# Sync queue of a gated cross-attention kernel: the load of the next second half of the stacks stands ahead of the store of the second half's maxima

## The reference, cut to what matters

```
q = rope(Wq @ layernorm(x) + bq); k = rope(Wk @ ctx + bk); v = Wv @ ctx + bv     # (16, 8, 512, 16) each
p = softmax(q k^T / sqrt(16)); x = x + tanh(g0) * (Wo @ (p v) + bo)
h = silu(layernorm(x) @ Wgate) * (layernorm(x) @ Wup); y = h @ Wdown
x = x + tanh(g1) * y / rms(y)
```

## Time and profile before

| | value |
|---|---|
| median of three runs | 773.88 us |
| profiled execution | 772.05 us, of which 770.2 us are the span from the first to the last instruction |
| TensorE | 697.0 us busy, 90% of the span |
| VectorE, ScalarE, GpSimd | 611.6, 524.3 and 471.9 us busy |
| DMA | 84.79 MB, mean 110 GB/s; the attention stage moves 150 to 219 GB/s in most slices |
| load of a half, one of its two transfers | 384 KB, 60 issues, median 6.3 us from issue to landing |

### The profile page before, as it was taken

How to read it: one execution, slowest core, us unless ns; L and a number is a source line. 1 busy time by engine, 2 the same in 40 slices (tenths; PEclk the granted TensorE clock), 3 DMA queues, 4 the chain that set the end, 5 groups by cost and what they waited for, 6 DMA issues and landing times. The chain is left out here.

```text
span 770.2 us, 13361 instructions
## 1 busy us (share of the span) xinstructions
PE 697.0 (90%) x4660; PEld 337.8 (44%) x4660; DVE 611.6 (79%) x822; ACT 524.3 (68%) x929; POOL 471.9 (61%) x399
## 2 busy tenths in 40 slices
PE   3589999989999999999999914899999999999995
PEld 1234443433444334433444303456655655565553
DVE  6689988859888889878888206877789888987894
ACT  2038888858888888878888813666675667566663
POOL 3935675656667866786421102796679668866762
PEclk9559999979999999999999966999999999999998
DMA  6787777877777787776851132000000200000011
GB/s 219 195 199 182 175 163 195 202 175 179 199 188 179 176 200 187 192 159 150 199 109 45 38 112 102 0 1 1 1 0 15 97 0 1 29 29 0 2 42 68
DMA packets 51047, 84.79 MB, mean 110 GB/s; under 512 B 14500, under 2 KB 17956, under 8 KB 50980
## 3 DMA queue, kind: packets, MB, share of 16 engines
q1 hardware_dynamic: 49680, 82.93, 42.5%
q10 hardware_dynamic: 1300, 1.01, 0.5%
HBM read 47.21 MB, written 34.34 MB: 106 GB/s over the span
## 5 line engine op out<-in xcount | busy, mean ns | idle before, releaser
L695 DVE TENSOR_REDUCE max_rows<-s_ps 128x2 f32<-128x1024 f32 x256 | 306.2, 1214 | 56.4 <-PE s_ps L440 55.2
L542 ACT ACTIVATE probs<-st_ps 128x512 f32<-128x512 f32 x512 | 277.4, 595 | 74.1 <-PE st_ps L452 64.0
L1088 ACT ACTIVATE parts<-gu_ps,gu_sc 128x512 f32<-128x512 f32 x176 | 118.0, 685 | 86.0 <-PE gu_ps L1176 85.9
L470 PE MATMUL pv_ps<-probs,v_ones 128*32 128x256 f32 x2048 | 164.9, 395 | 2.2 <-ACT pv_sb L548 2.2
L1062 POOL TENSOR_TENSOR pair<-parts 128x512 f32<-128x512 f32 x88 | 119.1, 1356 | 75.9 <-ACT parts L1088 75.5
L440 PE MATMUL s_ps<-qk_stack 48*128 48x512 f32 x512 | 134.6, 523 | 15.3 <-DMA qk_stack<-image 7.7
L1176 PE MATMUL gu_ps<-x_head,gu_bits 128*128 128x512 f16 x352 | 134.1, 381 | 4.1 <-DVE up L940 1.8
L1176 PE MATMUL gu_ps<-x_rest,gu_bits 128*128 128x512 f16 x352 | 133.4, 379 | 0.0
L452 PE MATMUL st_ps<-qk_stack 50*128 50x512 f32 x512 | 109.6, 417 | 0.5 <-DMA qk_stack<-max_scratch 0.4
L943 DVE SCALAR_TENSOR_TENSOR up<-gu_ps,gu_sc,up 128x512 f32<-128x512 f32 x132 | 98.8, 748 | 9.5
L440 PEld LDWEIGHTS s_ps<-qk_stack 48*128 48x128 f32 x512 | 50.0, 192 | 124.9 <-issue 76.5
(11 more groups left out here) (103 smaller groups left out, 852.0 us busy)
## 6 DMA issues: line engine op xcount, KB each, us to landing
qk_stack<-image SPq DMA_DIRECT2D x60, 384.0 KB, 6.3
image<-split_head SPq DMA_DIRECT2D x31, 256.0 KB
image<-split_head SPq DMA_DIRECT2D x62, 128.0 KB
image<-split_rest SPq DMA_DIRECT2D x31, 256.0 KB
ct<-ctx_dram SPq DMA_DIRECT2D x16, 256.0 KB, 4.3
scale_of<-inverse_scratch SPq DMA_DIRECT2D x16, 256.0 KB
xg<-x_scratch SPq DMA_DIRECT2D x4, 1024.0 KB, 7.2
out_dram<-y_out SPq DMA_DIRECT2D x16, 256.0 KB, 2.0
```

Of the source, the lines that this page charges most:

```text
L470: last = nc.tensor.matmul(pv_ps[2 * KC * j:2 * KC * (j + 1), cols], v_ones[b % 2][:, kt, j, quad, :], probs[at % PROBS][:, j, cols], start ...
L542: nc.scalar.activation(probs[at % PROBS][:, tile % 4, :], st_ps[item % ST_BANKS][:], ACT.Exp).then_inc(st_read, 1)
L695: nc.vector.tensor_reduce(out, s_ps[item % S_BANKS][:], AXIS_X, ALU.max).then_inc(s_read, 1)
L1088: nc.scalar.activation(parts[T_ % 2][:, k], gu_ps[(2 * k) % BANKS][:], ACT.Copy, scale=gu_sc[:, k, T_ % IT:T_ % IT + 1]).then_inc(gate_rea ...
```

## The change

In `sync_step` the store of the maxima of half 1 changes places with the load of half 1 of the next element. No instruction is added or taken away; the waits go with their functions.

```
 def sync_step(sp, b):
     nxt, proj_n = b + 1 < B, b + AHEAD_PROJ
-    store_max(sp, b, 1)
     if nxt:
         load_half(sp, b + 1, 1)
+    store_max(sp, b, 1)
     if b:
         gather_sums(sp, b - 1, 1)
     load_max(sp, b, 1)
```

## The result

The changed kernel takes 811.13 us (median; 805.21 to 818.34), against 773.19 us before: a ratio of 1.043 (95% interval 1.035 to 1.050), 33 us slower on 772. The forecast of 798 us had the sign, the place and the mechanism of the late store; the loss, 33 us by the ratio and 38 us by the medians, is 8 to 13 us larger than its 24.8 us. The time stays 0.9 us under the upper end of the stated range and lies just outside the 784 to 811 us of the forecast's own case: that it is inside the range at all is partly luck.

A forecast was written before the change was run, and what follows sets the result against it. A ring of sync queue and GpSimd, turning once per step, was taken as the bound. Seven turns (18.9 us), two with weight loads (2.8) and other steps (3.1) add 24.8 us to 772.05; with 1.8 for the median, 798 us, range 779 to 812.

The forecast's parts named there:

- the forecast's own case: Whole kernel: slower through the store's late return, forecast 798 us, own range 784 to 811 us, chance 0.62.
- The ring: Sync queue and GpSimd wait on each other, one turn per step, steps 3 to 12; a turn gets 2.7 us longer.
- The store behind the load: Sync queue: the store returns only once the load ahead has landed, so the load of the maxima goes 5.8 us late.
- The rival in which the store overtakes the load: Sync queue: store back before the load lands, its delay falls into idle time; 768 us (764 to 774), chance 0.09.
- The rival of a load that is quick once it is first: Sync queue: load lands within 4.5 us, store back at about 210.5; 768 us, chance 0.03.
- What the queue swallows: Sync queue, step 6: idle times of 2.26 and 1.51 us absorb part of the delay; broadcast issued 2.1 us late.
- The failed step: Sync queue, from the store of the inverses to the broadcast into `scale_of`: almost no gap, broadcast issued 2.1 us late.
- The open term: Landing of the broadcast into `scale_of`: 2.7 us late, between 2.1 us and 3.6 us.
- the second end: Broadcast landing set by the load of the first half, if bytes queued behind it keep engines full: 3.6 us late.
- the first rival: TensorE: its clock falls too after longer waits, five falls bring 798 to 808; 802 to 816 us, chance 0.12.
- Its counterargument: TensorE at slot 8: against a clock fall, the wait splits into two, at `score` and at `weigh`.
- Ahead of and behind the turns: Steps 12 and 13 add 1.3 us each at slot 8, step 2 some 0.5 us: 3.1 us.

The follow-up runs named there:

- experiment 8: Kernel before, with the load of the down scales moved behind the next step's load of the second half's maxima: 767.90 us, ratio 0.989.
- experiment 7: Changed kernel, with the load of the down scales moved behind the next step's load of the second half's maxima: 785.54 us, ratio 1.018 to the kernel before.
- experiment 9: Kernel before, with the load put first in steps 0 to 2 and 13 to 15 alone, old order in steps 3 to 12: ratio 1.002.
- experiment 4: Changed kernel, with the store of the second half's maxima issued from ScalarE's queue, behind the exponentials of slot 1: 780.16 us, ratio 1.001 to the kernel before.
- experiment 12: Kernel before, store first, with an added sync queue wait for the second half's load to land before the load of the maxima: 817.14 us, ratio 1.043.
- experiment 5: Changed kernel, with the load of the second half's maxima moved behind the merges and input loads: 812.84 us, ratio 1.038 to the kernel before.
- experiment 6: Changed kernel, with the store of the inverses moved ahead of the load of the first half: 816.02 us, ratio 1.050 to the kernel before.
- experiments 3: Changed kernel, with four throw-away products before the wait for the maxima at slot 8 of steps 3 to 13: 803.79 us, ratio 1.032 to the kernel before.
- experiment 10: Changed kernel, with four throw-away products before each of the two waits at slot 8 of steps 3 to 13: 806.75 us, ratio 1.035 to the kernel before.
- experiment 2: Changed kernel, with the store of the maxima placed between the load's two transfers: 791.33 us, ratio 1.013 to the kernel before.
- experiment 1: Changed kernel run again with no edit: 810.79 us, ratio 1.042 to the kernel before.
- experiment 11: Kernel before, load of the down scales moved as in experiment 8, two weight loads moved to steps 13 and 14 behind the input loads: 759.90 us, ratio 0.977.

## Why the prediction was right, and where it was short

*The ring.* Shown from both sides, for a third to a half of the loss: opening it gains 1.1% without the change (experiment 8) and brings the reorder's price from 4.3% down to 2.3 or 2.9% (experiment 7 against 8); the reorder outside it costs nothing that shows (experiment 9). The forecast put nearly the whole loss on the ring. With the ring open the queue's own issues and waits fill a step of 26.5 us, and that it did not see.

*The store behind the load.* Right in place and size: the load of the maxima was put 5.8 us late, and is 8.15 less 2.37, 5.8 us late (3.7 to 6.6 us over the nine turns, each against the same step before). The rival in which the store overtakes the load is out: in three of the nine turns the load of the maxima leaves 0.3 to 0.7 us before the load's second transfer has landed, in the other six 0.2 to 0.3 us after it. From another queue the store comes back no earlier when the load stands ahead of it (experiment 4). The rival of a load that is quick once it is first is out too: 7.5 us, as before. The Trainium skill gives the fit that the forecast set beside it ("DMA: Bandwidth & Descriptors", "Anatomy of one DMA") for transfers issued from GpSimd, and the load goes out on the sync queue, so the row decides. By experiment 12 the late load of the maxima, with the queue standing still ahead of it, is enough to explain the whole ratio. The Trainium skill, "DMA: Bandwidth & Descriptors", section "Queues, rings and completion order", gives each of the two issuing queues its own rings on the same 16 engines, each consumed in order, with the engines taking turns between rings. From that one would expect a store on the other queue to come back ahead of the load; the trace of experiment 4 does not show it, within 0.5 us in all six steps.

*What the queue swallows.* The store of the next maxima is 3.5 us late (3.6 forecast), the store of the inverses 2.3 us (2.1). The second agreement hides another cause. In the kernel before, this store left 0.03 us behind VectorE's reciprocals in all nine turns, so that the idle time ahead of it was a wait for TensorE, by way of VectorE, and no slack of the queue. The reciprocals in step 6 before (the store at 217.75), and in step 7 of the changed kernel (the store at 256.47):

```profile
217.38 0.34 DVE L714 RECIPROCAL sums<-sums 128x32 f32<-128x32 f32 x1
```

```profile
256.10 0.34 DVE L714 RECIPROCAL sums<-sums 128x32 f32<-128x32 f32 x1
```

In the changed kernel the reciprocals release this store in four of the nine turns (steps 4, 7, 8 and 10), and the queue's own order in the other five. The forecast let TensorE's lateness at slot 8 cost nothing inside the ring; it is a second path nearly as long as the queue's. In experiment 5 it releases the store in all nine turns, and nothing is gained.

*The failed step* is "From there to 222.94 the queue issues almost without a gap, so the broadcast is issued 2.1 us late". It is issued 3.8 us late (3.6 us against the same step, 7, of the kernel before). The broadcast waits until the store of the inverses has landed, and that store stands directly behind the load of the first half: the very rule that I had read off for the maxima, on a second pair of transfers. The wait on L297 has grown from 4.7 to 18.3 us, and goes when that store stands ahead of the load (experiment 6). What VectorE's wait had paid for is so taken back.

*The open term*, the broadcast's landing, came out between its two ends, 2.9 us late (25.01 us into the step, where it was 22.08) against the 2.7 us taken, though for another reason: late by its issue, and then quicker to land (4.1 us, not 4.93). That is luck too. Experiment 6 speaks for the second end: bytes queued ahead, not the issue. GpSimd starts 11.3 to 12.5 us after the issue of the load of the first half in the nine turns of the changed kernel, and 11.3 to 12.9 us after it before.

*The size.* Nine turns were forecast at 21.7 us and make 27.4 us. Three of the turns at full clock, 2.1 to 2.6 us longer, are the ring as it was forecast. The other six are 0.6 to 5.9 us longer. The two turns that begin behind a weight load were priced at 1.4 us each and cost 0.6 and 3.7 us (30.39 against 29.83, 30.34 against 26.66). Five turns fell under a clock of 1.00 where one had, the first rival, with its chance of 0.12. Its counterargument did not hold: the clock fell though the wait was split into 1.57 and 1.75 us (step 7), and in step 11 behind a single wait of 1.61 us. What the falls cost is not shown. Steps 7, 9 and 11, at 0.76 to 0.82, are 3.4 to 3.6 us longer than before; but in them the load of the maxima also left later, 8.2 to 8.9 us into the step, where it left after 7.3 to 7.4 us in the three turns at full clock. That alone can explain the difference, and the falls may follow from it. The 29.81 us turn, itself at full clock, follows one at 0.76; in it the queue waited 2.8 us for VectorE's maxima, from 337.08 to 339.92 us, as TensorE came late to slot 7, and here a cost of the clock is most likely. If all nine turns had cost 2.3 us, they would make 21 us; so some 6 us in the turns are what the later returns of the store and the clock make together, an estimate from these rows. How they divide stays open: experiments 3 and 10 point to the clock by 5 to 8 us, but within their intervals, and held it in neither.

*Ahead of and behind the turns* 3.1 us were forecast and 8.1 us measured. Step 14, which the forecast put at nothing, takes 2.7 us of them (24.32 us against 21.61 us); the rest was not taken apart.

## What to carry to other kernels

Ask of every transfer that is moved on a queue who on that same queue waits for its landing, and what now lies ahead of it: a small store behind a big load costs the load's whole flight to the instruction that waits, and to all behind it, and another queue does not save it. Apply that rule to every pair of transfer and wait in the turn, not to the moved pair alone. Before a second path is called free, ask what the idle time ahead of each transfer waits for. When a pace is set by a ring, look for the link that needs nothing from this turn, here a load of scales, and take it out: that gained 1.1%, and 2.3% with the weight loads moved to where little is queued, while the new order of load and store lost 4.3%.

## What the runs showed of the hardware

A transfer of 16 KB issued behind 768 KB came back 6.8 to 8.9 us after the load's first issue (10.5 and 10.6 us where a weight load stood ahead as well), behind 384 KB after 5.4 to 6.6 us (experiment 2, seven turns), and alone after 1.94 us. Issued from the other queue behind the load, it came back with the load's landing too (experiment 4, within 0.5 us in six steps). In five turns of the changed kernel TensorE's granted clock fell to the lower of its levels behind waits at slot 8, one of 5.5 us and the others of 1.1 to 1.8 us, alone or two in a row; in the kernel before it did not fall behind a wait of 1.50 us in step 11. The executions compared in experiment 1 lie between 805 and 815 us, those of the kernel without such waits (experiment 11) within 2.1 us. Four products on 48 rows in front of each wait did not keep the clock up (experiment 10: 0.94 from 170 to 440 us).
